# The first layer of a two-layer float32 kernel: sums of weights between two squares, bank copies in front of casts, outputs' weights sooner

## The reference, cut to what matters

```python
x = L0_attn_hidden_states                 # (8, 256, 512), float32
xn = layernorm(x)
x = x + attn0(xn) + ffn0(xn)              # attn0: linear attention, 32 heads of 128; ffn0: 16 experts, 2 chosen, one shared
xn = layernorm(x)
x = x + attn1(xn) + ffn1(xn)

# attn0
qkv = silu(xn @ qkv_w.T)                  # q, k, v for each head
scores = (q @ k.T) * decay                # causal, decayed, over 256 tokens
attn = rms_norm(scores @ v) * norm_w
attn0 = (sigmoid(xn @ gate_w.T) * attn) @ out_w.T
```

## Time and profile before

| | us |
|---|---|
| median of 3 runs | 2635.07 |
| lowest and highest | 2628.55, 2638.32 |
| profiled execution | 2639.82 |
| its span, first to last instruction | 2638.0 |
| PE busy | 2516.1 |
| POOL, VectorE, ScalarE busy | 1507.3, 1162.0, 1147.9 |
| mean granted clock of PE, share of full speed | 0.986 |

### The profile page before, as it was taken

How to read it: one execution, slowest core, us unless ns; L and a number is a source line. 1 busy time by engine, 2 the same in 40 slices (tenths; PEclk the granted TensorE clock), 3 DMA queues, 4 the chain that set the end, 5 groups by cost and what they waited for, 6 DMA issues and landing times.

```text
span 2638.0 us, 39435 instructions
## 1 busy us (share of the span) xinstructions
PE 2516.1 (95%) x13338; PEld 2147.9 (81%) x13338; DVE 1162.0 (44%) x1937; ACT 1147.9 (44%) x2182; POOL 1507.3 (57%) x1523
## 2 busy tenths in 40 slices
PE   7999999999999999989999999999999989969999
PEld 6888888888888887778888888888888878857777
DVE  6333333434333434753333333434343478865453
ACT  5444444444444444433444434344444357733332
POOL 4755756556565654756575757566575568731210
PEclk9999999999999999999999999999999999989999
DMA  4211111111111112211111110211111068831110
GB/s 162 84 47 40 53 62 37 54 46 60 38 53 46 54 39 96 84 46 54 40 54 38 54 60 31 62 46 54 38 60 41 25 234 296 300 121 48 32 33 32
DMA packets 84950, 188.00 MB, mean 71 GB/s; under 512 B 12610, under 2 KB 30674, under 8 KB 84870
## 3 DMA queue, kind: packets, MB, share of 16 engines
q1 hardware_dynamic: 76326, 170.13, 19.5%
q0 software_dynamic: 8544, 16.82, 2.1%
HBM read 168.00 MB, written 26.79 MB: 74 GB/s over the span
## 4 chain that ended last, share of the span: by engine, by line
PE 48%; issue 20%; POOL 18%; DVE 7%; ACT 5%; DMA 2%; POOLq 1%; ACTq 0%; SPq 0%; DVEq 0%
PE bank L95 13%; PE bank L97 13%; PE bank L96 13%; POOL wl L1809 6%; PE bank L1064 3%; PE bank L1081 3%; POOL w_in L492 3%; POOL w_in L494 2%; POOL w_in L496 2%; POOL w_in L498 2%; POOL sqacc L1823 2%; DVE el L2199 2%; PE bank L1082 1%; PE bank L1065 1%; POOL ol L1817 1%
## 5 line engine op out<-in xcount | busy, mean ns | idle before, releaser
L1809 POOL TENSOR_TENSOR wl<-w_in,wh 128x512 fp32r<-128x512 f32 x510 | 582.2, 1171 | 142.2 <-ACT wh L1348 137.4
L95 PE MATMUL bank<-xh,wh 128*128 128x512 f32 x1400 | 564.3, 403 | 37.5 <-ACT bank L1296 37.5
L97 PE MATMUL bank<-xh,wl 128*128 128x512 f32 x1400 | 549.9, 393 | 0.0
L1823 POOL TENSOR_TENSOR sqacc<-sqacc,sq 128x512 f32<-128x512 f32 x128 | 165.0, 1289 | 535.9 <-ACT sq L1333 522.8
L1348 ACT CAST wh<-w_in 128x512 fp32r<-128x512 f32 x502 | 263.3, 566 | 370.2 <-POOL w_in L498 370.2
L95 PEld LDWEIGHTS bank<-xh,wh 128*128 128x128 f32 x1400 | 264.6, 189 | 96.7 <-ACT bank L1296 44.2
L96 PE MATMUL bank<-xl_sums,wh 128*128 128x512 f32 x800 | 317.8, 397 | 0.0
L97 PEld LDWEIGHTS bank<-xh,wl 128*128 128x128 f32 x1400 | 264.3, 189 | 58.1
L1606 DVE TENSOR_TENSOR acc<-bank,acc 128x512 f32<-128x512 f32 x240 | 165.8, 691 | 304.8 <-PE bank L97 304.8
L95 PE MATMUL bank<-wh,xh 128*128 128x256 f32 x912 | 261.2, 286 | 10.2 <-DVE bank L1569 6.9
L96 PE MATMUL bank<-wl,xh 128*128 128x256 f32 x912 | 258.1, 283 | 0.0
(11 more groups left out here) (354 smaller groups left out, 5388.4 us busy)
## 6 DMA issues: line engine op xcount, KB each, us to landing
w_in<-in_w_pairs_dram SPq DMA_DIRECT2D x100, 512.0 KB, 3.8
o_in<-in_o_pairs_dram SPq DMA_DIRECT2D x32, 512.0 KB, 4.7
eraw<-in_ex_dram SPq DMA_DIRECT2D x31, 513.0 KB, 5.0
y_slots<-ey SPq DMA_DIRECT2D x31, 512.0 KB
w_in<-in_w_pairs_dram SPq DMA_DIRECT2D x56, 256.0 KB, 3.0
dcur<-in_decay_dram SPq DMA_DIRECT2D x32, 384.0 KB, 2.9
eraw<-in_ex_dram SPq DMA_DIRECT2D x31, 256.0 KB, 4.8
out_dram<-acc SPq DMA_DIRECT2D x16, 256.0 KB, 2.0
```

Of the source, the lines that this page charges most:

```text
L95: pe.matmul(out, wh, mh, start=start and i == 0, stop=False, skip_group_check=True)
L97: ins = pe.matmul(out, wl, mh, start=False, stop=stop and i == n - 1, skip_group_check=True)
L1809: pool.tensor_tensor(wl[:, cols], w_in[:, cols], wh[:, cols].bitcast(F32), ALU.subtract).then_inc(w_lo, 1)
L1823: pool.tensor_tensor(sqacc[:, c], sqacc[:, c], sq[:], ALU.add).then_inc(p_sq, 1)
```

## The change

It moves steps, and adds and takes away none.

1. POOL: `low` is cut in two, `add` (wait for the transfer, make the four sums) and `low` (the low parts). `add` for `q` (in `even` rounds `v1`) now stands between the squares 2 and 3, its `low` behind square 3 as before. `add_low` does both where they stood together.
2. ScalarE, `even` rounds, the two sections of values: the copy `t5` comes before the first cast, the eviction `a` before the second and third, and the fourth cast goes behind the eviction `b`.
3. `first` round: the two casts of `oh` stand before the evictions `c` and `b` and so before the casts of `k`; POOL does `low_o` before the sums and low parts of `k`. `SPLIT`, `READY` and `o_ready` follow: `second` waits for two more counts before its section 1, and SP for four fewer before it brings the next `o_in`.

```diff
-             "first": {"q": 4, "k": 8, "o": 10}, "second": {"g": 4, "v": 6, "q": 10, "k": 14, "o": 16},
+             "first": {"q": 4, "o": 6, "k": 10}, "second": {"g": 4, "v": 6, "q": 10, "k": 14, "o": 16},
...
-    READY = {"second": (-6, -2, 4, 6), "even": (-6, -2, 4, 12), "odd": (-4, 0, 4), "end": (-6, -2)}
+    READY = {"second": (-6, 0, 4, 6), "even": (-6, -2, 4, 12), "odd": (-4, 0, 4), "end": (-6, -2)}
...
-        return self.splits - (8 if self.odd else 0)
+        return self.splits - (8 if self.odd else 4 if self.second else 0)
...
                     take(r, 2, "e")
+                    if not r.first:
+                        wait(a, pe_out, r.n * 8)
+                    split_o(r.n, 0)
+                    take(r, 2, "c")
+                    split_o(r.n, 1)
+                    take(r, 2, "b")
                     if r.first:
-                        take(r, 2, "c")
-                        take(r, 2, "b")
...
                         split(r, "k", 2, 3)
-                        for i in range(2):
-                            split_o(r.n, i)
-                        return
-                    wait(a, pe_out, r.n * 8)
-                    split_o(r.n, 0)
-                    take(r, 2, "c")
-                    split_o(r.n, 1)
-                    take(r, 2, "b")
...
                         for j, what in ((3, "q"), (4, "k")):
                             take(r, j, "ab")
+                            take(r, j, "t5")
                             split(r, what, 0)
-                            take(r, j, "t5")
+                            take(r, j, "a")
                             split(r, what, 1, 2)
-                            take(r, j, "a")
-                            split(r, what, 3)
                             take(r, j, "e")
                             take(r, j, "c")
                             take(r, j, "b")
+                            split(r, what, 3)
...
+                def add(r, what, half=h):
+
+                    place = r.place(what)
+                    pool.wait_ge(dma_w[place], (r.arrived(what) * 16) + half * TOTAL[f"dma_w{place}"])
+                    add_up(pool, place, p_comb, r.summed(what) - 4 + half * TOTAL["p_comb"])
+
...
+                def add_low(r, what, half=h):
+                    add(r, what, half)
+                    low(r, what, half)
...
                     if r.first:
-                        low(r, "q")
-                        low(r, "k")
+                        add_low(r, "q")
                         low_o(r)
+                        add_low(r, "k")
...
                     add_squares(u, 2)
                     if sends:
                         send(1)
+
+                    add(r, "v1" if r.even else "q")
                     add_squares(u, 3)
                     if r.even:
                         low(r, "v1")
                     else:
                         low(r, "q")
-                        low(r, "k")
+                        add_low(r, "k")
```

More of the change, by code:

```diff
@@ L1797, in gpsimd @@
             def gpsimd(pool):
+                def add(r, what, half=h):
+                    place = r.place(what)
+                    pool.wait_ge(dma_w[place], (r.arrived(what) * 16) + half * TOTAL[f"dma_w{place}"])
+                    add_up(pool, place, p_comb, r.summed(what) - 4 + half * TOTAL["p_comb"])
                 def low(r, what, half=h):
-                    place, before = r.place(what), half * TOTAL["w_hi"]
                     pieces = 2 if what == "v" else 4
-                    if pieces == 4:
-                        pool.wait_ge(dma_w[place], (r.arrived(what) * 16) + half * TOTAL[f"dma_w{place}"])
-                        add_up(pool, place, p_comb, r.summed(what) - 4 + half * TOTAL["p_comb"])
                     for i in range(pieces):
-                        pool.wait_ge(w_hi, r.split(what) + (before - pieces + i + 1))
-                        cols = piece(place, i)
+                        pool.wait_ge(w_hi, r.split(what) + (half * TOTAL["w_hi"] - pieces + i + 1))
+                        cols = piece(r.place(what), i)
                         pool.tensor_tensor(wl[:, cols], w_in[:, cols], wh[:, cols].bitcast(F32), ALU.subtract).then_inc(
                             w_lo, 1)
+                def add_low(r, what, half=h):
+                    add(r, what, half)
+                    low(r, what, half)
                 def low_o(r):
@@ L1847, in run @@
                         refill.sums(pool)
-                        low(FRONT[1], "q", 1)
-                        low(FRONT[1], "k", 1)
+                        add_low(FRONT[1], "q", 1)
+                        add_low(FRONT[1], "k", 1)
                         return
                     if r.first:
-                        low(r, "q")
-                        low(r, "k")
+                        add_low(r, "q")
                         low_o(r)
+                        add_low(r, "k")
                         if last:
@@ L1869, in run @@
                     if r.even:
-                        low(r, "g")
+                        add_low(r, "g")
                         add_squares(u, 1)
@@ L1877, in run @@
                     if r.even:
-                        low(r, "v0")
+                        add_low(r, "v0")
                     if sends:
@@ L1935, in gpsimd @@
                     low(FRONT[1], "v")
-                low(FRONT[h], "g")
+                add_low(FRONT[h], "g")
                 all_rounds(pool, run)
```

## The result

The changed kernel took 2573.23 us (median of 4 runs, 2570.18 to 2574.90), beside 2634.24 us for the kernel before in the same comparison. The ratio is 0.9769, 95% interval 0.9748 to 0.9789: 61 us less, or 2.3%. Forecast were 2577 us. The profiled execution of after took 2570.18 us with a span of 2568.3; that of before 2639.82 with 2638.0. So the two traces differ by 69.6 us, and it is against this difference that the 62.5 us of the sum have to be held.

The account below looks back on a forecast made before the run. PE, busy 95% of the span, was held by waits for ScalarE's bank copy and VectorE's sum, and clock falls. 40.1 + 14.5 + 9.1 - 1.2 = 62.5 us off 2639.8 gives 2577 us; range 2565 to 2593.

Parts of the forecast that it names:

- Part 1: Second and odd rounds: sums of q ahead of the fourth square end PE's 16 waits for the bank copy; 40.1 us.
- Rival (b): The 16 stalls for the bank copy only shrink, to 0.5 to 1 us each; 2590 us, chance 0.08.
- The clock: Behind nine of the 16 stalls PE's clock falls; without the stalls 63 matmuls are won back, 14.5 us.
- Rival (a): The falls of the clock stay, brought on by shorter waits; 2591 us, chance 0.07.
- Part 2: Even rounds, sections 3 and 4: bank copies before casts end PE's 14 waits for VectorE's sum in a bank; 9.1 us.
- Rival (d): Even rounds: the late fourth cast delays sums of k and eviction a, so PE waits; slower, to 2653 us, chance 0.02.
- the 451.5: Even rounds: forecast time at which the sums of k end behind the late fourth cast, instead of 449.0.
- Part 3: First round, outputs' weights sooner: 1.2 us lost once in half 0 (bounds 0 and 3), nothing in half 1.
- The rule against the change: Second round, half 1: moved sums of q may hold up VectorE's small routing operations; bounds 0 and 3 us, taken 0.

Follow-up runs that it names:

- two lengthened casts: Changed kernel, ScalarE's casts of q lengthened in second and odd rounds: second cast cut in 32, 2593.70 us; first in 16 and second in 32, 2631.18 us.
- the kernel with 48 casts: Changed kernel with the first cast of q cut in 16 and the second in 32, in second and odd rounds: 2631.18 us.
- the run with 64 pieces: Changed kernel with POOL's subtraction for the fourth piece of q in even rounds cut in 64 of 4 columns: 2645.11 us.
- the run without the overlap: Changed kernel with POOL's order in the first round as in the kernel before, ScalarE's new order kept: 2564.77 us, ratio 0.9719.
- 32 narrow casts: Changed kernel with the second cast of q in second and odd rounds cut in 32 casts of 16 columns: 2593.70 us.
- bank copies alone: Kernel before with only ScalarE's reordering in sections 3 and 4 of even rounds (copy t5 first, fourth cast last): 2621.25 us, ratio 0.9938.
- outputs' weights alone: Kernel before with only the first round's casts of oh and subtractions for ol moved ahead of the sums of k: 2641.13 us, ratio 1.0013.
- the kernel with the copy first: Kernel before with ScalarE's bank copy ahead of the two casts of q in second and odd rounds, POOL's order untouched: 2590.65 us, ratio 0.9816.

## Why the prediction was right, point by point

**Part 1.** Right in mechanism and size. The step that carried it was that the sums wait for their place in POOL's queue, not for their transfer: with the sums ahead of the fourth square the casts follow the last eviction at once, and 40.1 us forecast stand against 40.1. The 2.43 us per stall was exact in half 0; in half 1 it was 2.4 to 2.8. The room behind it was set at 1.4 us; the rows have 1.6, and two lengthened casts agree (1.27 and 2.65 lost where 1.6 of room gives 1.22 and 2.60). Rival (b), a stall that only shrinks, is out with that.

**The clock.** Right: 14.5 forecast, 14.2 in the traces for nine falls fewer, 1.6 us each. That the falls hang on the stalls and not on something near them was argued in the prediction; the lengthened casts show it. Rival (a) is out. How large the gain is hangs on the execution: behind 16 full stalls before and its relatives had 9, 9 and 5 falls, and the kernel with 48 casts had 8. The prediction took this pair's nine, so the agreement to 0.3 us holds for this pair and for no other.

**Part 2.** 9.1 us forecast, 9.1 in the traces. The sums of `k` were to end 6.2 us before the next section is asked for (451.5 and 457.7) and end 6.3 before it: POOL, timeline of after.

```profile
440.85 0.74 POOL L498 TENSOR_TENSOR w_in<-w_in 128x256 f32<-128x256 f32 x1
```

They end at 441.59, PE asks at 447.89. Rival (d) had its place and its room right (5.0 us named, 5.05 read) and didn't come because every term of the 451.5 held; the run with 64 pieces shows what it does when one doesn't.

**Part 3.** Half right. In half 0 the 1.2 us were 0.98: ScalarE cast `k` at 77.31 and copied at 79.19, PE started at 79.81. The wrong step was "in half 1 ...: nothing". It weighed only when ScalarE's casts of `k` come. It should also have followed POOL's low parts of `k`, the 4.6 us later that the prediction itself worked out, to what runs beside them on VectorE. The timeline of after, POOL, VectorE and PE:

```profile
1094.00 4.67 POOL L1805 TENSOR_TENSOR wl<-w_in,wh 128x512 fp32r<-128x512 f32 x4 [0.73 <-ACT wh L1348]
...
1094.16 1.16 DVE L241 TENSOR_TENSOR acc<-acc 128x16 f32<-128x16 f32 x1
1095.36 1.22 DVE L242 TENSOR_SCALAR acc<-acc 128x16 f32<-128x16 f32 x1
...
1098.82 0.67 PE L1081 MATMUL bank<-ms,vt 128*128 128x256 f32 x2 [0.81 <-DVE ms L1559]
```

**The rule against the change.** It had the right mechanism and looked at the wrong place. At the place named, the sums of `q` in `second`, VectorE's chain L288 to L293 was indeed held up: L288 and L290 took 0.59 us where they took 0.18, L293 1.09 where it took 0.68, so 1.2 us in all, under the bound of 3; PE didn't wait, as taken, and the 3 us that the page's rule would have cost didn't come. The loss came where the same rule acts through part 3, 0.97 us. The Trainium skill, page "SBUF — State Buffer", section "SBUF: two separate sides", has VectorE and GpSimd take turns on one port pair for whole instructions; on VectorE's side it names those with two SBUF inputs and those in a mode that uses two ports. Two operations of 0.18 us that take 1.17 and 1.22 beside subtractions of 1.29 agree with that, and the run without the overlap gives the time back. Which mode L242 ran in, with its one input, no trace shows.

**The missing term.** The sum had no row for the matmul behind the first one after a stall. It comes 0.33 or 0.34 instead of 0.23 us later (498.74 in the earlier trace rows is such a first one), behind the 14 short stalls, where the matmuls have half the width, 0.22 instead of 0.12, and with 30 stalls gone this is 3.2 us. With it the sum would be 65.7, against 66.1 in the rounds.

**The median.** The prediction took the slow profiled execution, 2639.8, for one with more falls of the clock and held on to 2577. The medians differ by 61.0 us where the traces differ by 69.6, 5.6 us of it since this execution was above before's median and 3.1 since that of after was the fastest of its four. So the profiled pair overstates the gain. The 2577 came out 4 us above the median because the sum was taken off an execution 5 us slower than the median then known; off that median, 2635.07, it would have given 2572.6. The reason for leaving it there was wrong as well: the spread of before was read as more or fewer falls. A fall takes 0.28 off the granted clock of a window of 6 us, and so some 0.0006 off the mean over 2638 us; seven fewer would raise the mean by 0.004. In the 30 other executions of before, 2631 to 2643 us, it stays between 0.984 and 0.987 and doesn't follow the time: 0.986 in the fastest (2631.24), 0.984 at 2635.10, 0.987 at 2641.07. What makes those times differ is not known.

## What to carry to other kernels

When a consumer in one engine's queue waits for a producer in another's, look at what stands ahead of that producer in its own queue: here one moved line on POOL brought 59 to 63 us, and moving the consumer instead 49, with 14 new waits. When a step is moved, follow each of its instructions to the new time and ask what the neighbour on the same memory port does just then, small operations above all. Price a stall from start to start, and add the slower matmul behind it and the clock's fall, which in the rounds came only behind stalls of 2.4 us and more.

## What the runs showed of the hardware

TensorE's clock fell from its upper level (2.4 GHz) to 1.2 GHz behind stalls that interrupt steady work, and how often went with how long the stall was. In these kernels, time lost from start to start, and falls behind the stalls:

| kernel | lost at each | stalls | falls behind them |
|---|---|---|---|
| 32 narrow casts | 1.27 | 16 | 0 |
| bank copies alone | 2.43 to 2.8 | 16 | 5 |
| outputs' weights alone | 2.43 to 2.8 | 16 | 9 |
| before | 2.43 to 2.8 | 16 | 9 |
| 48 narrow casts | 2.65 | 16 | 8 |
| 64 narrow subtractions | 3.83 | 14 | 14 |

Nor did it fall behind the 28 waits of 0.5 to 1 us in the kernel with the copy first. Why a stall of 2.4 to 2.8 us brings a fall at one place and none at the next stays open here. Nor is one long stall the only thing that a fall can follow: at the end of half 1 in after the clock fell at 2054.6 us, behind waits of 0.92 and 0.46 us, sixteen matmuls of one column and the start of a third wait.

Small operations cost by their number: 16 casts of 32 columns in place of one of 512 added 1.4 us, 0.09 each, and 64 subtractions of 4 columns took 9.71 us, 0.15 each.
